# Keys of five batches of a second cross attention projected ahead, between the instructions of two earlier stages

## The reference

```python
# layer 0
x = x + xattn(k=ctx, v=ctx, q=layernorm(x), mask, L0 weights)   # 16 heads of 16
x = x + linear_attn(layernorm(x))      # softmax features, causal prefix sums
x = x + int8_ffn(layernorm(x))         # scale = sigmoid(clip) * max|x| / 127, over ALL of x
# layer 1
x = x + xattn(k=ctx, v=ctx, q=layernorm(x), L1 weights)
x = x + causal_attn(layernorm(x))
x = x + fp4_ffn(layernorm(x))
# in xattn: kh = ctx @ Wk.T + bk;  vh = ctx @ Wv.T + bv;  softmax(qh kh / 4) vh @ Wo.T + bo
```

## Time and profile before

| | us |
|---|---|
| median of 3 runs (lowest, highest) | 1440.49 (1436.46, 1441.02) |
| the profiled execution: its time | 1439.05 |
| its span, first to last instruction | 1437.0 |
| linear attention, from its first instruction to that of the next stage | 524.8 to 641.1 |
| int8 feed-forward | 641.1 to 705.4 |
| second cross attention, steps 0 to 63 begin | 732.1 to 1204.7 |

### The profile page before, as it was taken

How to read it: one execution, slowest core, us unless ns; L and a number is a source line. 1 busy time by engine, 2 the same in 40 slices (tenths; PEclk the granted TensorE clock), 3 DMA queues, 4 the chain that set the end, 5 groups by cost and what they waited for, 6 DMA issues and landing times. The chain is left out here.

```text
span 1437.0 us, 27170 instructions
## 1 busy us (share of the span) xinstructions
PE 1292.4 (90%) x10721; PEld 889.9 (62%) x10722; DVE 951.7 (66%) x1662; ACT 784.4 (55%) x1315; POOL 662.1 (46%) x352
## 2 busy tenths in 40 slices
PE   6999999999999967964599999999999998698497
PEld 3666666667667655632256667666766765587365
DVE  4685776765566644957657766775775655587786
ACT  4766666666666634533366566666666564354111
POOL 2755665666665632400145655665565455530000
PEclk9999999999999989987599999999999999899698
DMA  5312112112111010000310011001001000000000
GB/s 164 101 48 66 45 45 66 45 52 83 45 45 46 1 42 1 1 1 0 111 34 31 31 40 71 31 31 51 31 30 60 31 1 2 26 1 1 0 11 19
DMA packets 17084, 55.29 MB, mean 38 GB/s; under 512 B 2752, under 2 KB 8896, under 8 KB 12736
## 3 DMA queue, kind: packets, MB, share of 16 engines
q1 hardware_dynamic: 16960, 53.56, 11.7%
HBM read 52.51 MB, written 1.05 MB: 37 GB/s over the span
## 5 line engine op out<-in xcount | busy, mean ns | idle before, releaser
L525 POOL TENSOR_TENSOR ca_prob<-ca_prob,ca_inv_sum 128x1024 f32<-128x1024 f32 x256 | 493.2, 1948 | 380.0 <-DVE ca_inv_sum L758 380.0
L598 PEld LDWEIGHTS bank<-ident,ca_prob 128*128 128x128 f32 x2048 | 238.4, 141 | 92.3 <-issue 69.4
L638 ACT ACTIVATE ca_kT<-bank,ca_bk 64x512 f32<-64x512 f32 x256 | 174.9, 683 | 215.6 <-PE bank L537 213.8
L598 PE MATMUL bank<-ident,ca_prob 128*128 128x128 f32 x2048 | 266.9, 274 | 11.4 <-POOL ca_prob L525 6.2
L537 PE MATMUL bank<-ca_ctxT,ca_wk 128*128 128x512 f32 x512 | 244.8, 603 | 20.1 <-DMA ca_bk<-in_L_xattn_bk 17.1
L549 PE MATMUL bank<-ca_wv,ca_ctxT 128*128 128x256 f32 x1024 | 254.5, 392 | 0.0
L549 PEld LDWEIGHTS bank<-ca_wv,ca_ctxT 128*128 128x128 f32 x1024 | 184.3, 189 | 82.5 <-issue 59.5
L722 DVE CUSTOM_DVE_ANT_0 ca_neg_logit<-bank,ca_mask_add 128x1024 f32<-128x1024 f32 x128 | 151.6, 1222 | 112.5 <-PE bank L588 81.4
L725 DVE TENSOR_REDUCE ca_neg_max<-bank 128x1 f32<-128x1024 f32 x128 | 150.7, 1219 | 110.2 <-PE bank L588 110.2
L668 ACT ACTIVATE ca_prob<-ca_neg_logit,ca_neg_max 128x1024 f32<-128x1024 f32 x128 | 146.9, 1149 | 72.7 <-DVE ca_neg_max L722 72.7
L668 ACT ACTIVATE ca_prob<-bank,ca_neg_max 128x1024 f32<-128x1024 f32 x128 | 142.8, 1115 | 65.9 <-DVE ca_neg_max L725 65.9
(11 more groups left out here) (264 smaller groups left out, 1332.6 us busy)
## 6 DMA issues: line engine op xcount, KB each, us to landing
ca_ctxT<-in_ctxT SPq DMA_DIRECT2D x32, 1024.0 KB, 5.1
ca_mask_i<-in_mask SPq DMA_DIRECT2D x32, 256.0 KB, 4.8
lat<-in_x SPq DMA_DIRECT2D x1, 1024.0 KB, 4.8
out<-lat SPq DMA_DIRECT2D x8, 128.0 KB, 1.9
la_w_qkv<-in_L_attn_w_qkv SPq DMA_DIRECT2D x1, 768.0 KB, 3.9
ca_wi_raw<-in_L_ffn_w_down SPq DMA_DIRECT2D x1, 704.0 KB, 6.6
ca_fw_raw<-in_L_ffn_w_down SPq DMA_DIRECT2D x1, 704.0 KB, 6.3
ca_wi_raw<-in_L_ffn_w_gate SPq DMA_DIRECT2D x1, 640.0 KB, 5.0
```

The costliest lines, as they stand in the source:

```text
L525: pool.tensor_tensor(self.prob[:, x, :], self.prob[:, x, :], self.inv_sum[:, x:x + 1].broadcast_to([P, CTX]), ALU.mult).then_inc(self.norm ...
L598: tr = pe.transpose(self.core.bank[:, x, n * P:(n + 1) * P], self.prob[:, 2 * (s % 2) + p, (4 * h + n) * P:(4 * h + n + 1) * P], self.core ...
L638: op = act.activation(self.kT[half * S:(half + 1) * S, b % 2, 2 * m + r, :], self.core.bank[r * S:(r + 1) * S, x, :], ACT.Identity, bias=s ...
```

## The change

The keys of batches 0, 4, 8, 12 and 14 of the second cross attention are no longer made in its own block. A new class, `EarlyKeys`, makes them in 40 pieces (eight for each batch) of 128 x 256, half as wide as a `project_k`. PE's `project` uses banks 6 and 7 in turn, ACT's `take` copies a piece with its bias into a ring of four tiles, SP's `store` writes it to DRAM in two DMAs of 64 rows, and loads the next half batch of context (512 KB) after every fourth piece. Six pieces stand at the start of the linear attention and 34 in the int8 feed-forward. In the second cross attention these batches have no `project_k` and no `take_k`; SP's `load_k` reads their keys from DRAM (1 MB), once the stores are through and the scores of the batch two before are done, and `scores` waits for it. The four projections ahead of step 0 are now those of batch 1.

With it come other edits. The weights of the linear attention are loaded at the end of the first stage (`LinearWeights`). Its values use banks 0 to 3, one of them stands ahead of the feature map, the map ahead of `z` 4, and ACT's copies follow that order. POOL makes `dist` of tile t + 1 ahead of `feat` of tile t. In the int8 feed-forward the small matmuls move from banks 6 and 7 to 4 and 5, and the down projections use six banks. `load_ctx(sp, 0)` moves ahead of the key weights, in the second cross attention it stands behind the value weights, and `project_v` waits for the context itself.

```diff
+class EarlyKeys:
+    BATCHES = (0, 4, 8, 12, 14)
+    PIECES = 8
+    RING = 4
+    BANKS = (6, 7)
...
+    def load_ctx(self, sp, g):
+        if g >= 2:
+            sp.wait_ge(self.projected, 4 * (g - 1))
...
+    def store(self, sp, count):
+        for n in range(self.sent, self.sent + count):
...
+            sp.wait_ge(self.taken, n + 1)
+            half, first = part // 2, part % 2 * D
+            for r in range(2):
+                sp.dma_start(self.store_at[b, half * S:(half + 1) * S, 2 * m + r, first:first + D],
+                             self.out[r * S:(r + 1) * S, n % self.RING, :]).then_inc(self.stored[n % self.RING], 16)
+            if n % 4 == 3 and n // 4 + 2 < 2 * len(self.BATCHES):
+                self.load_ctx(sp, n // 4 + 2)
...
+    def project(self, pe, count):
+        for n in range(self.put, self.put + count):
+            m, g, part = (n // 2) % 2, n // 4, n % 2
+            if n == 0:
+                pe.wait_ge(self.w_loaded, 32)
+            if n % 4 == 0:
+                pe.wait_ge(self.ctx_loaded[g % 2], 16 * (g // 2 + 1))
+            if n >= 2:
+                pe.wait_ge(self.taken, n - 1)
+            for k in range(KD):
+                mm = pe.matmul(self.core.bank[:, self.BANKS[n % 2], 0:D], self.wk[:, k, m * P:(m + 1) * P],
+                               self.ctxT[:, g % 2, k, part * D:(part + 1) * D], start=(k == 0), stop=(k == KD - 1))
+            mm.then_inc(self.projected, 1)
...
+    def take(self, act, count):
+        for n in range(self.copied, self.copied + count):
+            act.wait_ge(self.projected, n + 1)
+            if n >= self.RING:
+                act.wait_ge(self.stored[n % self.RING], 32 * (n // self.RING))
...
 class CrossAttention:
+    def load_k(self, sp, b):
+        e = self.early_batches.index(b)
+        self.early.wait_stored(sp, e)
+        if b >= 2:
+            sp.wait_ge(self.scores_ready, GROUPS * (b - 1))
+        sp.dma_start(self.kT[:, b % 2, :, :], self.early.store_at[e, :, :, :]).then_inc(self.k_loaded, 16)
...
 def linear_attention(core, weights, early):
+            distances(0)
+            for t in range(TILES):
+                if t + 1 < TILES:
+                    distances(t + 1)
                 pool.wait_ge(inv_ready, t + 1)
...
+            early.project(pe, LA_PIECES)
...
+            pe.wait_ge(early.taken, LA_PIECES)
+            for n in range(4):
+                queries_and_keys(n)
+            values(0)
+            pe.wait_ge(z_taken, 4)
+            feature_map(0)
+            queries_and_keys(4)
+            feature_map(1)
+            for n in range(5, 8):
+                queries_and_keys(n)
+            for t in range(1, TILES):
+                values(t)
...
+            early.take(act, LA_PIECES // 2)
             ln.on_scalar(act)
+            early.take(act, LA_PIECES - LA_PIECES // 2)
...
+FILL_NORM, FILL_SCALE, FILL_TRANSPOSE, FILL_MAX, FILL_INT, FILL_END = 11, 3, 2, 4, 4, 3
+FILL_UP = (2, 4, 6, 8, 10)
 def int8_ffn(core, weights, early):
         def _(act):
+            early.take(act, FILL_NORM // 2)
             ln.on_scalar(act)
             act.wait_ge(clip_loaded, 32)
             act.activation(sig[:, :], clip[:, :], ACT.Sigmoid).then_inc(sig_ready, 1)
+            early.take(act, FILL_NORM - FILL_NORM // 2)
...
         def _(pe):
+            early.project(pe, FILL_NORM)
             pe.wait_ge(wide_ready, KD)
...
             spread_maximum(0)
+            early.project(pe, FILL_SCALE)
...
+            early.project(pe, FILL_MAX)
             spread_maximum(1)
+            early.project(pe, FILL_INT)
...
+            early.project(pe, FILL_END)
...
 def second_cross(core, ffn_weights, early):
             for n in range(4):
-                ca.project_k(pe, n, n)
+                ca.project_k(pe, 4 + n, n)
...
-                if s + 4 < STEPS:
+                if 8 <= s + 4 < STEPS and (s + 4) // 4 not in early.BATCHES:
                     ca.project_k(pe, s + 4)
```

197 lines of the change are left out of this document (137 added, 60 removed).

## The result

The changed kernel takes **1416.96 us** (median; 1414.59 to 1417.77) against 1440.52 for the kernel before beside it, a ratio of 0.984, 95% interval 0.982 to 0.985. The prediction was 1415.5 with a range of 1403 to 1428. The total is right, in part by luck: of its terms, the second cross attention came out 1.9 us lower with its opening, the linear attention 1.0 lower, the int8 stage 3.4 higher, and the first layer, for which nothing was forecast, 1.7 higher. The low terms (-2.9) and the high ones (+5.1) nearly cancel: the profiled execution came 2.4 above its forecast (1416.74 for 1414.35), the median 1.5.

What follows compares the result with a forecast made beforehand. PE was taken to bound the second cross attention (busy 453.4 of 455.6 us). Terms -26.8 - 1.2 + 3.3 = -24.7 on 1439.05 gave 1414.35, with 1.44 for the median 1415.8, stated as 1415.5, range 1403 to 1428.

Steps and rivals of the forecast that it cites:

- Second cross attention, -26.8: Second cross attention: removing the keys of five batches saves PE time, -26.8 us, bounds -34.2 to -22.2.
- Steps 0 to 3: Opening steps of the second cross attention: step 0 saves nothing, steps 1 to 3 save 3.8 us together.
- Window 52 to 55: Four steps without keys in the second cross attention, two even saving 1.71 us each, two odd 1.17: 5.76 in all.
- Linear attention, -1.2: Linear attention stage: later root, fewer waits for ACT and a longer loop sum to -1.2 us, bounds -5 to +3.
- a turn: Loop of the linear attention: `feat` queued behind `dist` on POOL lengthens each pass from 8.50 to 9.2 to 9.25 us.
- Int8 feed-forward, +3.3: Int8 feed-forward stage: 34 pieces delay its opening and closer sums shorten its tail, +3.3 us, bounds 0 to +9.
- The last three pieces, a copy and two stores end with POOL.: End of the int8 stage: the final pieces and their stores finish with POOL's sums, in a tail of -1.1 us.
- the eleventh: Int8 opening: this piece waits for a context load issued at 12.0, landing in 3.3; PE reaches L1421 6.0 us later.
- Every projection in full: Rival, chance 0.14: each removed key projection saves its full time, cross attention -34.2, earlier stages -4 and +1: 1403 us.
- The pieces are paced by transfers: Rival, chance 0.20: late stores make a piece take 1.5 us, not 1.06; some 26 pieces cost 11 more: 1427.
- The clock falls: Rival, chance 0.04: PE's clock drops in cross-attention steps without keys, making the kernel slower, 1534 us if in all.

## Why the prediction was right, and where it was not

**Second cross attention, -26.8.** Measured -27.9 in the steps and -0.8 in the opening. Steps 0 to 3 gave 4.0 us (predicted 3.8), and step 0 still ends on ACT: 4.84 for 4.85. Window 52 to 55 gave 5.8, as said. The other three gave 6.0 to 6.1 (12 to 15: 6.62, 5.29, 7.06 and 5.46 us, for 8.35, 6.46, 8.78 and 6.90): an odd step in which PE has further work gave 1.44 instead of 1.17. With the 0.2 of steps 0 to 3 that is the 1.1 us. No step waited for the keys read from DRAM.

**Linear attention, -1.2.** Measured -2.2. The root came at 6.3 us (6.8 said), `z` 2.0 later (1.8 said), the first feature transposes at 35.0 (34.4 said), a turn took 9.27 (9.2 to 9.25 said). The kernel before itself swings by 2 us in this stage, so this term can't be judged closer. Its structure can: the kernel with the old POOL order shows that the new order costs 3.1 in the loop, for which I had 3.6.

**Int8 feed-forward, +3.3.** Measured +6.7. Here one step failed, and it is "The last three pieces, a copy and two stores end with POOL." POOL's last sum came 66.9 us after the stage's start against 63.5, that is +3.4, what the whole sum had given. But the next stage then started 4.2 us later instead of 0.9. The end of the changed kernel's stage, POOL, PE and SP:

```profile
702.03 5.52 POOL L1475 TENSOR_TENSOR lat<-qf_prod,lat 128x256 f32<-128x256 f32 x8 [83.11 <-DVE qf_prod L1544]
...
705.18 2.86 PE L270 MATMUL bank<-ek_ctxT,ek_wk 128*128 128x256 f32 x12
...
706.85 3.64 SPq L246 DMA_DIRECT2D early_k<-ek_out  x6
...
711.72 0.33 SPq L562 DMA_DIRECT2D ca_ctxT<-in_ctxT  x1
```

The three pieces can't start on PE before its last down projection has ended, at 705.2. They take 2.86 us, and the last copy ends at 708.55, 1.0 behind POOL. SP issues the six stores of the three pieces back to back from 706.85 to 710.49 (706.85 + 3.64), some 0.6 us each, where I had 0.43 from another row; that is 1.9 more. The next stage starts 1.2 behind that; before it started 0.9 behind POOL. So the larger part of the tail was the queue of stores. With the root ahead of the takes PE was through before POOL, and the overhang was 3.7 all the same. I had asked neither when the *first* of the three could start nor when SP would be through with the last.

Ahead of it the sum was right by luck, by errors that cancel. The opening on ACT and PE:

```profile
640.73 5.45 PE L270 MATMUL bank<-ek_ctxT,ek_wk 128*128 128x256 f32 x24 [1.44 <-PEq L101]
...
645.79 0.47 ACT L283 ACTIVATE ek_out<-bank,ek_bk 128x256 f32<-128x256 f32 x1 [0.83 <-DMA early_k<-ek_out]
...
647.57 0.21 ACT L162 ACTIVATE qf_std<-qf_var 128x8 f32<-128x8 f32 x1
...
650.19 7.46 PE L270 MATMUL bank<-ek_ctxT,ek_wk 128*128 128x256 f32 x20 [4.02 <-DMA ek_ctxT<-in_ctxT]
```
```profile
650.19:655.90 5.71, 5.71 (x13) 4.56 (x14) 3.90 (x8) 1.13 (x3) 0.00 (x0) 0.50 0.61 171
```

The pieces ran at full clock from the start (six in 5.45 us), so the root came at 6.9, not at 8.5. So PE came sooner to the seventh piece, whose context SP loads only behind the stores of the second; it landed 4.6 us after its issue began, and PE waited 4.02 us for it, till 650.19. I had such a wait only at the eleventh. Behind the wait the granted clock was 0.50 until 655.9 (the second fence), where I had taken full clock from the fourth piece on; so the eleventh piece came after its context had landed and waited for nothing. The first maximum was then 6.1 late, for 6.0. With half clock at the start, as in the kernel with one store a piece (root at 8.8), the first maximum came at 17.5, nearly the same. Even with no wait for a context at all it came at 16.6. Idle time on PE isn't what was lacking: eleven pieces at full clock are 9.5 us (11 x 0.86), and 10.2 of the 11.2 us were idle without them. What the pieces met there were ACT, whose copies share this stretch with the root, the sigmoid and two table loads, and half clock behind some of the waits (those of 4.02 and 2.21 us, but not the one of 2.24 with the root ahead). The price of each alone stays open.

**The rivals.** *Every projection in full* fell: odd steps gained 1.17 to 1.45. *The pieces are paced by transfers* had the pace nearly right, 1.43 us a piece on SP (two stores of 0.64, a fourth of 0.60) for its 1.5, and the price wrong: taking the stores away altogether gave back 2.0 us of the int8 stage, not 11, or some 3.2 if the last pieces had kept their clock (an estimate from 4.12 - 2.86). Most pieces had nothing due behind them. *The clock falls* fell: 1.00 in the steps without keys. The Trainium skill's rule that transposes don't count as matmuls do ("TensorE: Matmul & The Clock Gate", "Part 4: PE-mode transpose") would have put it lower there; in this case's mix of matmuls and transposes the trace shows nothing of it. As for its 1.38 us drain at a table load ("ScalarE: Activation LUTs", "What ACT_TABLE_LOAD costs"): the root's activation starts at 647.57, right behind the load of 1.28 us that starts at 646.28, and the load right behind the copy that ends at 646.26, so again the trace shows no drain.

## What to carry to other kernels

Work moved into another stage is free only where it stands *between* two events of the chain that bounds that stage. Here 16 pieces in the middle cost nothing, 11 at the head cost 6 us and 3 at the tail 3 us, and four more in the middle already cost 2.6. For each filler ask not only what it hides behind, but when it can start, what its copies and stores stand in line with, and which queue has the last word at the stage's end. A net of small losses and gains in stages that each swing by 1 to 2 us can't be settled by the total: read each stage's own boundaries.
